# Pacing the indirect transfers of three routed trees by the ring's own steps

## The reference

```python
def _fff(x, node_w, node_b, w1, b1, w2, b2):
    xf = x.reshape(-1, D)                      # 2048 tokens
    cur = zeros(N)
    for _ in range(4):                         # depth 4: 15 nodes, 16 leaves
        score = einsum('nd,nd->n', xf, node_w[cur]) + node_b[cur]
        cur = 2 * cur + 1 + (score >= 0)
    leaf = cur - 15
    return relu(xf @ w1[leaf] + b1[leaf]) @ w2[leaf] + b2[leaf]   # per token its own leaf

q, k, v = _fff(x, q...), _fff(x, k...), _fff(x, v...)
attn = softmax(einsum('bqd,bkd->bqk', q, k) / 16)
return einsum('bqk,bkd->bqd', attn, v)
```

## Time and profile before

| what | value |
|---|---|
| median of three timed runs | 1663.05 us (1657.81 to 1673.67) |
| span of the profiled execution, first to last instruction | 1738.4 us |
| the trees' scatters: 48 DMAs, first to last start | 1247.7 to 1307.6 us |
| the ring's outputs: 69 copies, first to last start | 1318.6 to 1461.8 us |
| gathers of tree 0, 16 DMAs, first to last start | 1357.9 to 1376.7 us |
| gathers of tree 1, 16 DMAs | 1410.5 to 1429.2 us |
| gathers of tree 2, 16 DMAs | 1464.8 to 1483.6 us |

### The profile page before, as it was taken

The page is one execution under the profiler, slowest core; times in us unless marked ns, Lnnn a source line. Parts: engine busy times, 40 slices in busy tenths (PEclk is TensorE's granted clock), DMA queues, the critical chain, the costliest instruction groups (busy, mean ns, idle before and its releaser), DMA issues. The chain is left out here.

```text
span 1738.4 us, 29519 instructions
## 1 busy us (share of the span) xinstructions
PE 1457.5 (84%) x9881; PEld 1174.3 (68%) x9882; DVE 692.5 (40%) x1864; ACT 637.5 (37%) x1415; POOL 485.4 (28%) x545
## 2 busy tenths in 40 slices
PE   4999979999999997899979899465917668767598
PEld 3566757799999975477768899443816546645487
DVE  3455524200000034477624000377404334449676
ACT  2344532244444422266623444221403234323343
POOL 2455440022222210423120222142270332121330
PEclk8999987999999999699989999777768789889799
DMA  5800006366666640000026466200434654010000
GB/s 177 228 2 1 2 1 200 106 201 200 198 201 200 199 140 3 1 2 2 2 66 217 135 201 200 85 1 0 150 129 133 197 152 145 22 49 1 0 18 30
DMA packets 111835, 173.73 MB, mean 100 GB/s; under 512 B 20315, under 2 KB 88557, under 8 KB 111225
## 3 DMA queue, kind: packets, MB, share of 16 engines
q1 hardware_dynamic: 101567, 144.26, 26.5%
q0 software_dynamic: 10176, 28.24, 4.6%
HBM read 133.06 MB, written 39.35 MB: 99 GB/s over the span
## 5 line engine op out<-in xcount | busy, mean ns | idle before, releaser
L686 DVE TENSOR_REDUCE nmax<-ps 128x2 f32<-128x512 f32 (+1 forms) x256 | 145.6, 617 | 122.2 <-PE ps L864 73.9
L1359 ACT ACTIVATE kT<-ps,b_sb 128x128 f32<-128x128 f32 x312 | 114.7, 368 | 155.7 <-PE ps L1476 134.6
L646 ACT ACTIVATE wbuf<-ps 128x512 f32<-128x512 f32 (+1 forms) x256 | 123.9, 542 | 91.3 <-PE ps L887 90.8
L1476 PEld LDWEIGHTS ps<-qT,wbuf 128*128 128x128 f32 x1248 | 145.4, 192 | 3.9 <-issue 1.9
L1476 PE MATMUL ps<-qT,wbuf 128*128 128x128 f32 x1248 | 145.7, 275 | 1.7 <-DVE x_tok L1182 1.7
L1486 PE MATMUL ps<-L0f_second,kT 128*128 x624 | 141.1, 379 | 0.0
L269 POOL TENSOR_TENSOR sm<-sm,mhalf 128x4 f32<-128x4 f32 (+1 forms) x40 | 43.8, 1095 | 325.4 <-DVE sm L264 325.4
L1486 PEld LDWEIGHTS ps<-L0f_second,kT 128*128 128x128 f32 x624 | 115.5, 190 | 14.1
L314 ACT ACTIVATE xnT<-ps 128x512 f32<-128x512 f32 (+1 forms) x64 | 37.1, 596 | 200.4 <-PE ps L310 95.4
L887 PE MATMUL ps<-nmT_r,sel_r 32*128 32x256 f32 (+1 forms) x512 | 109.3, 425 | 0.0
L1306 POOL DMA_INDIRECT qT<-expert_rows,rowt x39 | 38.0, 975 | 159.1 <-PE ps L1465 106.5
(11 more groups left out here) (444 smaller groups left out, 3121.8 us busy)
## 6 DMA issues: line engine op xcount, KB each, us to landing
wbuf<-in_L_w SPq DMA_DIRECT2D x66, 1024.0 KB, 8.8
tree_rows<-rt SPq DMA_DIRECT2D x3, 3151.0 KB, 28.6
prob<-tree_rows SPq DMA_DIRECT2D x69, 137.0 KB
tree_outputs<-probT SPq DMA_DIRECT2D x69, 128.0 KB
L0f_second<-in_L_w SPq DMA_DIRECT2D x8, 1024.0 KB, 10.7
ts<-in_L_b SPq DMA_DIRECT2D x58, 128.0 KB
wbuf<-in_L_rec SPq DMA_DIRECT2D x3, 2048.0 KB, 10.4
expert_rows<-vbuf SPq DMA_DIRECT2D x2, 2048.0 KB, 7.5
```

What stands on the lines that cost most here:

```text
L646: act.activation(PT[:, k, :, q0:], ps[:, a_bank("ST", b, k), :].rearrange("p (h s) -> p h s", h=2)[:, :, q0:], ACT.Exp, scale=scale).then_ ...
L686: ins = dve.tensor_reduce(nmax[:, b % 2, qt, h:h + 2], bank[:, :, 0:keys(qt)], AXX, ALU.max, negate=True)
L1359: act.activation(hs[:, f, :], hidden(f), func, bias=b1_sb[:, v, f:f + 1]).then_inc(h_in, 1)
L1476: ins = pe.matmul(hidden(f), first[v][:, kk, f * P:(f + 1) * P], xgT[:, kk, :], start=(kk == 0), stop=(kk == KD - 1))
```

## The change

The gathers, and the scatters of trees 1 and 2, each get a wait of their own. Tree 0's scatters stay back to back. Scatter t of tree 1 waits until the ring has made t - 3 outputs (the first four don't wait), scatter t of tree 2 until it has made 15 + t. Gather t of tree 0 waits for 33 + t outputs, gather t of tree 1 for 53 + t, besides the wait for all stores of the tree. Of the gathers of tree 2 the first four go at once, and each further four wait until one more block's scores have been computed. The weights of tree 2 come in 16 DMAs of 128 KB, one for each of the first 16 steps of tree 1, on SP between the step's store and the next load; ACT waits for all of them before the first step of tree 2.

```diff
+            PIECES = 16
+            PIECE = REC // PIECES
+            AHEAD, SECOND, BACK = -3, 15, (33, TOTAL - NT)
...
+                    def load_part(i):
+                        o = ds(i * PIECE, PIECE)
+                        sp.dma_start(wbuf[:, 0, o], a["L2_rec"][2, :, o]).then_inc(ld_w2[2], 16)
...
                         store(done)
-                        if isinstance(done.s, int) and done.r == 0 and done.s == TSTEPS - 1:
-                            load_tree(2)
+                        if done.r == 1 and (not isinstance(done.s, int) or done.s < PIECES):
+                            load_part(done.s)
...
-                    for r in range(TREES):
+                    for t in range(NT):
+                        scatter(0, t)
+                    for r, start in ((1, AHEAD), (2, SECOND)):
                         for t in range(NT):
-                            pool.indirect_dma_start(a[f"xt{r}"], ...
+                            wait(pool, y_out, t + start)
+                            scatter(r, t)
                     for r in range(TREES):
                         pool.wait_ge(sent[r], NT * 16)
-                    for r in range(TREES):
-                        for v in range(ROUND):
-                            pool.wait_ge(y_st[v], len(range(v, TSTEPS * (r + 1), ROUND)) * 16)
+                    for r, start in ((0, BACK[0]), (1, BACK[1])):
+                        outputs_stored(r)
                         for t in range(NT):
-                            pool.indirect_dma_start(out_tile(r, t), None, a[f"yt{r}"], ...
+                            pool.wait_ge(y_out, t + start)
+                            gather(r, t)
+                    outputs_stored(2)
+                    for t in range(NT):
+                        if t >= 4:
+                            pool.wait_ge(s_full, t // 4 * 2)
+                        gather(2, t)
                     for blk in range(NB):
                         nrm.power(pool, blk, 0)
...
-                            act.wait_ge(ld_w2[s.r], 16)
+                            act.wait_ge(ld_w2[s.r], 16 * (PIECES if s.r == 2 else 1))
```

More of the change, by code:

```diff
@@ L2531, in _, with scatter, gather @@
                     pool.wait_ge(zeroed, 48)
-                    for r in range(TREES):
+                    def scatter(r, t):
+                        pool.indirect_dma_start(a[f"xt{r}"], bass.IndirectOffsetOnAxis(rowt[:, t * TREES + r:t * TREES + r + 1], 0),
+                                                x_row(t), None).then_inc(sent[r], 16)
+                    def gather(r, t):
+                        pool.indirect_dma_start(out_tile(r, t), None, a[f"yt{r}"],
+                                                bass.IndirectOffsetOnAxis(rowt[:, t * TREES + r:t * TREES + r + 1], 0)).then_inc(got[r] if r < 2 else got_v[t // 4], 16)
@@ L2534, in _, with outputs_stored @@
+                    def outputs_stored(r):
+                        for v in range(ROUND):
+                            pool.wait_ge(y_st[v], len(range(v, TSTEPS * (r + 1), ROUND)) * 16)
+                    for t in range(NT):
+                        scatter(0, t)
+                    for r, start in ((1, AHEAD), (2, SECOND)):
                         for t in range(NT):
-                            pool.indirect_dma_start(a[f"xt{r}"], bass.IndirectOffsetOnAxis(rowt[:, t * TREES + r:t * TREES + r + 1], 0),
-                                                    x_row(t), None).then_inc(sent[r], 16)
+                            wait(pool, y_out, t + start)
+                            scatter(r, t)
@@ L2538, in _ @@
                     for r in range(TREES):
                         pool.wait_ge(sent[r], NT * 16)
-                    for r in range(TREES):
-                        for v in range(ROUND):
-                            pool.wait_ge(y_st[v], len(range(v, TSTEPS * (r + 1), ROUND)) * 16)
+                    for r, start in ((0, BACK[0]), (1, BACK[1])):
+                        outputs_stored(r)
                         for t in range(NT):
-                            pool.indirect_dma_start(out_tile(r, t), None, a[f"yt{r}"],
-                                                    bass.IndirectOffsetOnAxis(rowt[:, t * TREES + r:t * TREES + r + 1], 0)).then_inc(got[r] if r < 2 else got_v[t // 4], 16)
+                            pool.wait_ge(y_out, t + start)
+                            gather(r, t)
```

## The result

The changed kernel takes 1671.89 us, the median of 20 runs (1664.38 to 1682.24). The kernel before, run beside it 20 times, takes 1662.73 (1657.70 to 1674.29). The ratio is 1.0059, with a 95% interval of 1.0040 to 1.0078: some 10 us lost, inside the 1% within which I had put the outcome, and 1.9 above the 1670 predicted. The profiled execution, one of the 20, took 1682.24, which is 1.74 more than its span. It is so in every timed run whose span is on record, 365 in all: the time is the span and 1.69 to 1.81 us. Ahead of the prediction I had written that the timed runs are taken without a profile. That is wrong: the profiled execution is itself one of them, and of the others, too, span and clock are listed.

A forecast was written before the change was run, and what follows sets the result against it. It took PE's late signals around back-to-back indirect DMAs, 87.4 us, to hold the profiled trees' phase, mostly only while recorded. Bursts -4, weights -2 and +2, ring's end +1, power +10 gave +7: 1670 us, range 1618 to 1686.

The forecast's parts named there:

- the late power: Attention behind the ring: POOL's first power, queued behind gathers waiting for block 2's scores, costs 7.4 to 11.7 us, taken 10.
- Is that time in the timed runs?: Trees' phase: most lost time exists only while the execution is recorded; at most 12.0 us can be in the median.
- the 87.4 us: Trees' phase of the profiled execution: lost time priced at 42.0 before the first output, 18.5 and 17.6 at gathers, 9.3 behind.
- the hold-up: Trees' phase: PE's signals come late around back-to-back indirect DMAs, 87.4 us in the profiled execution.
- The first rival: Trees' phase: the hold-up is real in timed runs, so the change gives 1591 us, or 1627 if half won; chance 0.20.
- Bursts broken up: Scatters and gathers, one per ring step: gain 0 to 12.0 us, the median's share of the hold-up; taken 4.
- Waits on POOL in the ring: Ring: scatters and gathers waiting for outputs still leave early enough for the rows; cost 0.
- Weights in 16 parts: Ring, tree 1's steps: gain 0 to 2.6 us, taken 2; the parts' traffic costs 0 to 5.9, taken 2.
- The end of the ring: Behind the ring's last copy: PE waits for the last gather of keys; cost 0 to 4 us, taken 1.
- The powers behind the gathers of tree 2: Attention behind the ring: POOL's first power waits for block 2's scores, delaying DVE and PE; 7.4 to 11.7 us, taken 10.
- What the profile would show: Signs: first output at 1275 to 1290, span falling more than the median, power late, DVE idle 10 to 14 us.
- the vanished wait of L2697: First steps of tree 1: the wait for rows, 2.56 us before, was to be gone from the changed kernel's profile.

The follow-up runs named there:

- e4: Kernel before with only tree 2's weights in 16 parts, scatters and gathers still back to back: 1658.18 us, ratio 0.9967 to the kernel before.
- e9: Kernel before, unedited, profiled a third time, one run: 1674.31 us.
- e3: Kernel before with only the scatters of trees 1 and 2 and gathers of trees 0 and 1 paced: 1667.13 us, ratio 1.0034 to the kernel before.
- e5: Kernel before with the 16 gathers of tree 0 issued twice, PE waiting for both: 1663.12 us, ratio 1.0016 to the kernel before.
- e6: Changed kernel without the waits on scores ahead of the gathers of tree 2: 1661.75 us, ratio 0.9990 to the kernel before.
- e1: Changed kernel with block 0's power moved ahead of the last four gathers of tree 2: 1662.36 us, ratio 0.9994 to the kernel before.
- e2: Kernel before with only the waits on scores ahead of the gathers of tree 2 added: 1672.37 us, ratio 1.0068 to the kernel before.
- e7: Kernel before, unedited, profiled a second time, one run: 1660.86 us.
- e8: Changed kernel without the waits on scores, gathers of tree 0 two and of tree 1 six steps earlier: 1657.66 us, ratio 0.9964 to the kernel before.

## Why the prediction was right

The time was predicted at 1670 and measured at 1671.89, and the term that I held for the costliest, the late power, is the one that decides. Step by step, in the order of the prediction:

*Is that time in the timed runs?* That the 87.4 us are not in them was right, and it is what made the sign right: of the 65 timed runs of the kernel before whose span is listed, none takes longer than 1677.29. But my reason does not hold as I gave it. I held that recording an execution makes the hold-up. The timed runs have their spans on record as well, and 11 of the 12 profiled executions of this study, of nine kernels, have no hold-up: recording alone does not make it. The other clue that I used, a wait of ACT's L2577 put down to a transfer long ended, does not come again: in the second and third execution of the kernel before, the waits of this line end with PE's L2690. Landings of row loads are missing in seven of the twelve profiles, e4 and e9 among them, whose heads and rings are undisturbed; missing records of that kind are no mark of a hold-up. What held up that one execution stays open; so does whether a kernel with bursts is struck now and then and a paced one never, since one case in the six profiles with gathers in bursts and none in the six with paced ones can't tell.

The price was too high as well. The phase was longer by 323.1 less 244.0, the mean of the other two: 79.1 us, not 87.4. The head lost 40.1 (42.0 said), the ring 28.6 (36.1 said, at 1.52 us per output; an undisturbed ring takes 1.69, its stall included), the tail 10.3 (9.3 said). And 1.7 us lie around the span, not 12.0: 1738.4 - 79.1 + 1.7 = 1661.0, within 2.1 of the median, which leaves the bursts nothing in the timed runs.

The first rival, named beside the Trainium skill's Runtime: NRT & Kernel Launch (Instruction fetch mechanics), asked for a gain from pacing in timed runs too. e3, which paces, is slower; e5, with one burst more, is not slower by the 17 to 19 us that a burst should cost. No run here shows code that came late.

*Bursts broken up*, taken at -4 with 0 to -12: 0. Heads of 31.1 and 30.8, rings of 110.9 (paced) and 110.6 (e4, in bursts). I still gave the hold-up a part of the 12 us by which the spans' sum left room; nothing was there. Wrong by 4.

*Waits on POOL in the ring*, 0: right (115.7 in e3 against 114.6, within the spread).

*Weights in 16 parts*, -2 for the stall and +2 for the parts' traffic, 0 together: measured -3.7 in the ring (110.9 less 114.6), -4.0 in e4 alone, -5.5 (-10.1 to -0.8) in its timed runs. The stall was sized too small. I priced it at the wait of one row; its true price is the wait and the slower matmuls behind it, 3.40 and 6.3 in the execution shown above. The traffic of the parts was sized about right, 0.6 to 2.6 by the estimate beside e4, though PE never waits for rows. My 1.94 us of transfers per step were too many: the DMA engines were busy for 0.92 of 1.77 us, which is 1.63.

*The end of the ring*, 0 to 4, taken 1: the wait came as said, 3.00 us (I had said 1 to 3), but cost 2.6 by the tails of e6 and before, and 3.4 by the eleven traces beside e6. That the stores would cover it was wrong. Behind the wait, transposes and scores run at the lower clock in all five traces that have it, which I had not counted; they do so in some of the others too, as in e9.

*The powers behind the gathers of tree 2*, 7.4 to 11.7, taken 10: right. DVE idles 14.22 us (10 to 14 said), PE waits 7.52 (7.4 said), the maxima are 11.56 late (11.7 said). Its price: 9.8 between the tails of the changed kernel and e6, 10.8 by e1, 11.3 by e2 in the timed runs (6.1 in e2's one trace, against tails at another clock), each between kernels that differ in this alone.

The sum: 0 - 3.7 + 0.3 + 2.6 + 9.8 = +9.0 by the traces (0.3 is the head), where I had -4 - 2 + 2 + 1 + 10 = +7. The bursts are off by 4 us one way and the weights by 3.7 the other, the keys by 1.6. That the total comes so near is luck; the sign is owed to the power.

*What the profile would show.* The power behind the scores, the wait for keys and the vanished wait of L2697 came as said. Two signs were badly chosen. The first output at 1275 to 1290 (it is at 1289.2), and a span that falls by more than the median, hold for the kernel before as well, in its second execution: they tell that execution from others and say nothing of the change, nor of recording.

## What to carry to other kernels

An in-order queue charges a wait to everything behind it: before a wait goes in ahead of a transfer, look for the smallest instruction queued behind that transfer and for who waits for it, and move it up (10.8 us here for one power of 1.05 us). A large load on the queue that also brings the small tiles of a ring is better cut into parts of about their size; and a wait of the matmul engine is to be priced with the slower matmuls behind it (6.3 us here for a wait of 3.40), not by its own length. Where the profiled execution is far longer than the timed runs, have a second execution profiled before anything is explained from the first.

## What the runs showed of the hardware that I had not expected

- One execution of 12 profiled was some 80 us longer than others of the same kernel (phase 323.1 against 243.7 and 244.2), in stretches with indirect DMAs back to back, with PE's granted clock at 0.61 and 0.65 in the two runs of gathers. In the second execution of the same kernel the same DMAs leave the ring at 1.62 us per output with the DMA engines 0.85 busy.
- A short wait of PE can be followed by matmuls at half speed, the lower of the clock's two levels, and the same wait can differ from one execution to the next. Behind 7.52 us, eight transposes took 1.97 us. Behind 3.0 they took 1.94 in both executions of the changed kernel, but 1.06 to 1.21 in e1, e3 and e6, where the next eight took 1.97. Behind a wait of 1.40 they took 1.97 in e9 and 1.15 in e7, which are the same kernel. So the granted clock of the tail is 0.97 and 0.91 in two executions of the kernel before, 0.81 and 0.88 in two of the changed one, and 1.00 in e8.
- Sixteen loads of 128 KB beside loads of rows, stores and indirect DMAs, at a DMA share of 0.92 and 273 GB/s over their 16 steps, cost PE no wait for rows in any of six traces, while one load of the same bytes makes it wait 1.9 to 5.8 us in each of the six traces that have it.
